# Hybrid convolution, attention and expert kernel on one core: experts of a half in one run, GpSimd weightings and dummy matmuls, another order of scan stage and batch norm

## What is computed

```python
# layer 0: convolution and two Mamba scans, one in each direction over the 256 tokens of an image
o = silu(depthwise_conv3x3(lin1(x)) + dw_b)
s = tokens(o) @ fc_in_w
o = (mamba(s, 0) + flip(mamba(flip(s), 1))) @ fc_out_w
o = (o - mu) * rsqrt(var + 1e-5) * bn_g + bn_b         # batch norm over images and pixels
x1 = sigmoid(conv1x1(o, conv4_w) + conv4_b) * x + x
# layer 1: causal attention on 256 tokens of 32 channels, one head
t = t + attention(layernorm(t))
# layer 2: mixture of 8 experts, the best two for each token
h = layernorm(t)
p = softmax(h @ router_w + router_b); top_p, top_i = top_k(p, 2); top_p /= sum(top_p)
t = t + sum_k top_p[k] * (h @ expert_w[top_i[k]] + expert_b[top_i[k]])
```

## Time and profile before

| | us |
|---|---|
| median of three runs | 103.01 |
| the three runs | 103.29, 98.75, 103.01 |
| profiled execution | 99.49 |
| its span, first to last instruction | 97.7 |
| PE busy | 87.1 |
| weight loads (PEld) busy | 54.5 |
| DVE busy | 47.3 |
| ACT busy | 34.8 |
| GpSimd busy | 16.6 |

### The profile page before, as it was taken

The page is one execution under the profiler, slowest core; times in us unless marked ns, Lnnn a source line. Parts: engine busy times, 40 slices in busy tenths (PEclk is TensorE's granted clock), DMA queues, the critical chain, the costliest instruction groups (busy, mean ns, idle before and its releaser), DMA issues.

```text
span 97.7 us, 1958 instructions
## 1 busy us (share of the span) xinstructions
PE 87.1 (89%) x793; PEld 54.5 (56%) x793; DVE 47.3 (48%) x116; ACT 34.8 (36%) x76; POOL 16.6 (17%) x31
## 2 busy tenths in 40 slices
PE   5999999999969979766988978999979999998990
PEld 1424465544456645533637654665546676995980
DVE  1420041956679578335334830641157999991000
ACT  5001282962280145453697214347424010001011
POOL 5000990007429500000000000000000009000000
PEclk9999999999999999998599999999999655555589
DMA  2699600000000000000000000000000000000000
GB/s 53 216 277 345 247 7 0 0 0 0 0 7 0 7 0 0 0 0 7 3 3 0 0 0 0 7 0 0 0 0 0 0 7 0 0 27 27 0 27 27
DMA packets 1620, 3.16 MB, mean 32 GB/s; under 512 B 198, under 2 KB 838, under 8 KB 1612
## 3 DMA queue, kind: packets, MB, share of 16 engines
q1 hardware_dynamic: 1612, 3.04, 9.8%
HBM read 2.78 MB, written 0.26 MB: 31 GB/s over the span
## 4 chain that ended last, share of the span: by engine, by line
PE 79%; ACT 11%; DVE 3%; DMA 2%; issue 2%; DVEq 0%
PE banks L560 8%; PE banks L883 8%; PE banks L912 8%; PE banks L530 5%; PE banks L597 4%; PE banks L902 3%; PE banks L679 3%; PE banks L615 2%; DMA pw<-in_pw 2%; PE banks L652 2%; PE banks L901 2%; PE banks L522 2%; PE banks L515 2%; PE banks L746 2%; PE banks L666 2%
## 5 line engine op out<-in xcount | busy, mean ns | idle before, releaser
L1000 DVE TENSOR_TENSOR_SCAN lmat<-banks,data 128x512 f32<-128x512 f32 x8 | 9.7, 1217 | 4.5 <-PE banks L597 4.4
L324 POOL TENSOR_TENSOR lmat<-lmat 128x512 f32<-128x512 f32 x2 | 2.5, 1290 | 47.6 <-DVE lmat L1209 47.6
L912 PE MATMUL banks<-pb,lmat 128*128 128x128 f32 x40 | 8.3, 386 | 0.0
L560 PE MATMUL banks<-o,fold_w 32*32 32x512 f32 x128 | 8.2, 596 | 0.0
L912 PEld LDWEIGHTS banks<-pb,lmat 128*128 128x128 f32 x40 | 8.1, 302 | 0.0
L883 PE MATMUL banks<-pd,h 32*128 32x256 f32 x32 | 7.8, 563 | 0.1
L515 PE MATMUL banks<-warm 128*128 128x512 bf16 x15 | 5.9, 524 | 1.2 <-DVE warm L960 1.2
L883 PEld LDWEIGHTS banks<-pd,h 32*128 32x128 f32 x32 | 5.5, 268 | 1.1 <-issue 0.7
L1006 DVE TENSOR_TENSOR mmat<-banks,lmat 128x512 f32<-128x512 f32 x8 | 5.0, 682 | 1.3 <-PE banks L615 1.3
L482 ACT ACTIVATE fin<-banks 128x128 f32<-128x128 f32 x4 | 1.1, 277 | 12.2 <-PE banks L912 12.2
L1209 DVE TENSOR_TENSOR lmat<-banks,wtok 128x256 f32<-128x256 f32 (+1 forms) x12 | 5.4, 504 | 0.1
(11 more groups left out here) (185 smaller groups left out, 165.8 us busy)
## 6 DMA issues: line engine op xcount, KB each, us to landing
im<-in_im SPq DMA_DIRECT2D x2, 445.5 KB
pc<-in_pc SPq DMA_DIRECT2D x1, 577.5 KB, 7.7
pb<-in_pb SPq DMA_DIRECT2D x1, 405.0 KB, 6.8
pd<-in_pd SPq DMA_DIRECT2D x1, 336.0 KB, 8.1
x<-in_x SPq DMA_DIRECT2D x1, 256.0 KB, 7.8
out<-fin SPq DMA_DIRECT2D x4, 64.0 KB, 1.6
pw<-in_pw SPq DMA_DIRECT2D x1, 100.2 KB, 2.2
pf<-in_pf SPq DMA_DIRECT2D x1, 80.0 KB, 6.3
```

What stands on the lines that cost most here:

```text
L560: mm = pe.matmul(proj_bank[2 * d + g][to:to + C, :], fold_w[r, 2 * d + g, k, :], o4[r, :, at:at + L], start=(k == 0), stop=(k == TAPS1 - 1))
L912: mm = pe.matmul(o, mix[:, k, e, :, :], packs["ident"], start=False, stop=(e == terms - 1))
L1000: dve.tensor_tensor_scan(lmat[:, i, :], dab_bank[i % 2][:, :], data1[:, d, :], 0.0, ALU.mult, ALU.add).then_inc(S["scanned"], 1)
```

## The change

**Scan stage.** PE issues the prefix rows and both turns of the first group behind the last projection instead of between projections; ACT does all four silu before the two copies. `products(1)` stands ahead of the second output, `states(1)` behind it. The fourth output's square moves from ACT to DVE, and `mean_squares(3)` and `gated(3)` stand earlier. The folds of the output weights stand behind the products for dt.

**Batch norm.** DVE subtracts the mean while it reads PSUM (`centred_o`), in place of ACT's copies. The weights are multiplied by `bn_g` early, on GpSimd; the shift's product with `bn_b` stands ahead of the statistics. Dummies: six ahead of the average, six behind it, five behind the gate matmuls (before: one, one, five, three).

**Experts' stage.** The bias is written into the four banks by four matmuls of one row, and the eight matmuls of a half follow in one run, block by block over four images. ACT copies half 0's four banks to `eout` in SBUF; half 1 waits for the copies. DVE weights images 0 and 1 of half 0 from `eout`, GpSimd images 2 and 3 by four products of 128x256; GpSimd's additions go, and half 0's blocks have eight products each. The bias by turned weights goes. Ties among experts are found by a running count (a scan of 128x64 with a reset) and one instruction, in place of a product, a maximum and a comparison. 18 dummies stand between these matmuls. One input pack is 64 columns wider.

Core of the diff:

```diff
-            for k in range(NC):
-                pool.wait_ge(S["mix_ready"], BQ)
-                pool.tensor_tensor(mix[:, k, 0:E // 2, :, :], mix[:, k, 0:E // 2, :, :], mix[:, k, E // 2:E, :, :], ALU.add)\
-                    .then_inc(S["summed"], 1)
+            w4 = wtok[:, 0, :, :].rearrange("p (k q) e -> p k q e", q=BQ)
+            for q in POOL_MIX:
+                pool.wait_ge(S["e_copied"], q + 1)
+                pool.wait_ge(S["w_ready"], 1)
+                for k in range(NC):
+                    m = pool.tensor_tensor(mix[:, k, :, q, :], eout[:, q, k, :, :],
+                                           w4[:, k, q, :].rearrange("p (e o) -> p e o", o=1).to_broadcast([P, E, C]), ALU.mult)
+                m.then_inc(S["pool_mixed"], 1)
...
             silu(0)
             silu(2)
+            silu(1)
+            silu(3)
             turned_copy(0)
             turned_copy(1)
-            silu(1)
-            silu(3)
...
-            square(3)
             rms(3)
-            for bh in range(BH):
-                act.wait_ge(S["bn_stats_done"], bh + 1)
-                act.activation(osb[:, bh, :], o_bank[bh][:, 0:L], ACT.Copy).then_inc(S["o_copied"], 1)
...
+            def expert_copy(q):
+                act.wait_ge(S["e_done"], 1)
+                act.activation(eout[:, q, :, :, :].rearrange("p k e c -> p (k e c)"), e_bank[q][:, :], ACT.Copy)\
+                   .then_inc(S["e_copied"], 1)
...
             inverse_sums(1)
+            expert_copy(0)
             ln2_square(1)
+            expert_copy(1)
             ln2_root(1)
             second_exp(0)
-            w_copy(0)
+            expert_copy(2)
+            expert_copy(3)
             second_exp(1)
             store_copy(0)
             store_copy(1)
-            w_copy(1)
...
-            prefix_rows(0)
             project(1, 0)
-            transposed(0)
             decays(3)
             project(1, 1)
-            transposed(1)
             decays(4)
             project(1, 2)
             decays(5)
             project(1, 3)
+            transposed(0)
             decays(6)
+            transposed(1)
+            prefix_rows(0)
             products(0)
             decays(7)
             states(0)
             skipped(0)
             outputs(0)
             prefix_rows(1)
+            products(1)
             skipped(1)
             outputs(1)
-            products(1)
...
+            mean_squares(3)
             mixer_out(0, 0)
             mixer_out(0, 1)
-            mean_squares(3)
             mixer_out(1, 0)
-            keep_warm(1, 0)
             mixer_out(1, 1)
-            keep_warm(1, 0)
+            pe.matmul(bank[7][:, 4:5], packs["conv4"], packs["bn_b"], start=True, stop=True)
+            keep_warm(6, 0)
             pe.wait_ge(S["bn_step"], 2)
             pe.matmul(bank[7][:, 0:2], packs["bn_avg"], bn_mv[:, :], start=True, stop=True).then_inc(S["bn_avg_done"], 1)
-            keep_warm(5, 6)
-            pe.wait_ge(S["bn_shift_ready"], 1)
-            pe.matmul(bank[7][:, 2:3], packs["conv4"], bn_v[:, 4:5], start=True, stop=True).then_inc(S["shift_done"], 1)
+            keep_warm(6, 0)
             pe.wait_ge(S["conv4_w_ready"], 1)
             pe.wait_ge(S["m_ready"], 8)
             for bh in range(BH):
-                pe.wait_ge(S["o_copied"], bh + 1)
+                pe.wait_ge(S["o_centred"], bh + 1)
                 pe.matmul(bank[2 + bh][:, 0:L], conv4_w[:, :], osb[:, bh, :], start=True, stop=True)\
                   .then_inc(S["conv4_done"], 1)
-            keep_warm(3, 6)
+            keep_warm(5, 0)
...
-            def experts(j):
-                q, bh = j % BQ, j // BQ
-                r = slice(C * q, C * q + C)
+            def expert_bias(bh):
+                if bh == 0:
+                    pe.wait_ge(S["prob_ready"], 4)
+                else:
+                    pe.wait_ge(S["e_copied"], BQ)
+                for q in range(BQ):
+                    r = slice(C * q, C * q + 1)
+                    pe.matmul(e_bank[q][:, :], ones[r, :],
+                              packs["experts_b"][r, :].rearrange("p (o n) -> p o n", o=1).to_broadcast([1, NC, E * C]),
+                              start=True, stop=False)
+            def experts(bh):
                 pe.wait_ge(S["h2_ready"], bh + 1)
-                if j == 0:
-                    pe.wait_ge(S["prob_ready"], 4)
-                if j >= 4:
-                    pe.wait_ge(S["mix_ready"], j - 3)
-                for i in range(2):
-                    mm = pe.matmul(e_bank[q][:, 256 * i:256 * i + 256], h2[r, bh, Q * i:Q * i + Q],
-                                   packs["experts"][r, :], start=True, stop=True)
+                for c in range(NC):
+                    for q in range(BQ):
+                        r = slice(C * q, C * q + C)
+                        mm = pe.matmul(e_bank[q][:, 256 * c:256 * c + 256], h2[r, bh, Q * c:Q * c + Q],
+                                       packs["experts"][r, :], start=False, stop=(c == NC - 1))
...
+            def opened(k):
+                bh, c = k // NC, k % NC
                 pe.wait_ge(S["t2_ready"], bh + 1)
                 pe.wait_ge(S["rest_ready"], bh + 1)
-                r = slice(32 * (k % NC), 32 * (k % NC) + 32)
-                pe.matmul(o, packs["experts_b"][r, :], wtt[r, bh, :], start=True, stop=False)
-                pe.matmul(o, packs["ident"], t2[:, bh, Q * (k % NC):Q * (k % NC) + Q], start=False, stop=False)
-                terms = E // 2
-                if bh == 0:
-                    pe.wait_ge(S["summed"], k + 1)
+                pe.matmul(mixed_bank[k][:, 0:Q], packs["ident"], t2[:, bh, Q * c:Q * c + Q], start=True, stop=False)
...
+            def mixed(k):
+                terms = E
+                if k < NC:
+                    pe.wait_ge(S["mix_ready"], len(DVE_MIX))
+                    pe.wait_ge(S["pool_mixed"], len(POOL_MIX))
                 elif k == NBLK - 1:
                     pe.wait_ge(S["last_summed"], 1)
+                    terms = E // 2
                 else:
-                    pe.wait_ge(S["mix_ready"], 2 * BQ)
-                    terms = E
+                    pe.wait_ge(S["mix_ready"], len(DVE_MIX) + BQ)
                 for e in range(terms):
-                    mm = pe.matmul(o, mix[:, k, e, :, :], packs["ident"], start=False, stop=(e == terms - 1))
+                    mm = pe.matmul(mixed_bank[k][:, 0:Q], mix[:, k, e, :, :], packs["ident"], start=False,
+                                   stop=(e == terms - 1))
...
+            expert_bias(0)
+            experts(0)
+            pe.wait_ge(S["l2_ready"], 1)
+            keep_warm(1, 7)
             centre2(1)
+            keep_warm(3, 7)
             variance2(1)
-            experts(0)
+            keep_warm(5, 7)
+            route_bias(1)
+            route(1)
+            keep_warm(3, 7)
+            expert_bias(1)
             experts(1)
-            route_bias(1)
-            experts(2)
-            route(1)
-            experts(3)
-            weights_turned(0)
-            experts(4)
-            experts(5)
-            experts(6)
-            experts(7)
+            keep_warm(6, 7)
+            opened(0)
+            opened(1)
             mixed(0)
             mixed(1)
-            weights_turned(1)
+            opened(2)
+            opened(3)
...
+            gated(3)
+            dve.wait_ge(S["yg_ready"], 4)
+            dve.tensor_tensor(ysq[:, 1, 1, :], yg[:, 1, 1, :], yg[:, 1, 1, :], ALU.mult).then_inc(S["ysq3_ready"], 1)
             normed(1)
-            gated(3)
...
+            def centred_o(bh):
+                dve.tensor_scalar(osb[:, bh, :], o_bank[bh][:, 0:L], bn_m[:, 0:1], None, ALU.subtract)\
+                   .then_inc(S["o_centred"], 1)
+            centred_o(0)
+            dve.wait_ge(S["halved"], 1)
+            dve.scalar_tensor_tensor(bn_v[:, 5:6], bank[7][:, 4:5], 0.5, b_half[:, :], ALU.mult, ALU.add)\
+               .then_inc(S["bias_ready"], 1)
+            dve.wait_ge(S["conv4_g_ready"], 1)
             dve.wait_ge(S["bn_rs"], 1)
-            dve.tensor_tensor(bn_v[:, 3:4], packs["bn_g"], bn_v[:, 2:3], ALU.mult).then_inc(S["bn_scale_ready"], 1)
-            dve.wait_ge(S["bn_scale_ready"], 1)
-            dve.scalar_tensor_tensor(bn_v[:, 4:5], bn_m[:, 0:1], bn_v[:, 3:4], packs["bn_b"], ALU.mult, ALU.subtract)\
-               .then_inc(S["bn_shift_ready"], 1)
-            dve.tensor_scalar(conv4_w[:, :], packs["conv4"], bn_v[:, 3:4], None, ALU.mult).then_inc(S["conv4_w_ready"], 1)
-            dve.wait_ge(S["shift_done"], 1)
-            dve.wait_ge(S["halved"], 1)
-            dve.scalar_tensor_tensor(bn_v[:, 5:6], bank[7][:, 2:3], -0.5, b_half[:, :], ALU.mult, ALU.add)\
-               .then_inc(S["bias_ready"], 1)
+            dve.tensor_scalar(conv4_w[:, :], conv4_g[:, :], bn_v[:, 2:3], None, ALU.mult).then_inc(S["conv4_w_ready"], 1)
+            centred_o(1)
...
```

(11 more changed lines are left out.)

120 lines of the change are left out of this document (49 added, 71 removed), and 3 rows, old and new, of the table names.

## The result

The changed kernel takes 96.11 us (four runs, 95.85 to 96.42); the kernel before, on the same chip, 98.75 to 103.29 us (four runs, median 101.25). The ratio is 0.970, interval 0.962 to 0.978: faster by 3%. The kernel before has executions near 99 and executions near 103; every ratio in this document is taken over the shorter of the executions of either kernel, and the four runs here, as will turn out, are all of the changed kernel's longer kind. The profiled execution took 96.21 us, its span is 94.4.

What follows compares the result with a forecast made beforehand. PE, with 79% of the chain, bounds the kernel, and its half clock sets 17 us. Span 97.7 - 1.1 - 5.1 = 91.5, time 93.3, plus 1.0 for a short half-clock stretch: 94.3 us, range 91.3 to 98.7.

Steps and rivals of the forecast that it cites:

- the starting point of the sum: Whole kernel: the old profiled execution's span, 97.7 us, from which the gains were subtracted; 1.79 us lie around it.
- Rival 4: Whole kernel: executions of the kind of 103 us dominate, giving 97 to 98 us; chance 0.08.
- Scan stage: Scan stage: moved turns cost 0.8 us, the square on DVE saves 1.25; -0.2 to -0.5, counted as zero.
- The wait of 0.9 us ahead of the second transposition: Scan stage: PE waits there for the first turned copy; its absence would show the forecast wrong.
- Batch norm: Batch norm: earlier shift matmul and DVE centring bring the layer norm's first square from 51.09 to 50.0; -1.1 us.
- Experts' stage: Experts' stage to the last mixing product: ends at 90.3 instead of 95.43, -5.1 us, at full clock.
- weights to mixing: Experts' stage: from half 0's weights at 78.5 to the mixing's start at 83.5.
- The alternation: Weighting: DVE and GpSimd take turns reading SBUF operands; of GpSimd's 2.5 us, 2.0 are lost to DVE.
- rival 2: Experts' stage: clock falls at 76.3 as before, returns early in the mixing; 97.1 us, chance 0.17.
- The added 1.0 us for one short stretch at half clock: Whole kernel: allowance for one half-clock stretch as short as the batch norm's 3.5 us, raising 93.3 to 94.3.
- Rival 1: Weighting: no loss between DVE and GpSimd, mixing starts at 81.8, 1.7 earlier; 91.6 us, chance 0.07.
- Rival 3: Experts' stage to the end: the clock falls and stays low, slower, ending at about 102 us; chance 0.10.

Runs made afterwards that it cites:

- before_dense: Kernel before with only four full-row dummies added directly behind the convolution; median 100.07 us, ratio 1.012.
- before_dense_warm: Kernel before with four dummies behind the convolution and 15 in the experts' stage; median 94.36 us, ratio 0.954.
- dve_all: Changed kernel with DVE weighting all four images of half 0 and GpSimd none; 92.53 to 96.67 us, median 95.12.
- dense_no_dummies: Changed kernel with folds ahead of the dt products and four dummies behind the convolution, without the experts' stage's 18 dummies; median 94.65 us, ratio 0.960.
- before_warm: Kernel before with 15 dummies between its expert matmuls, nothing else changed; 100.46, 96.94, 92.74 and 94.61 us.
- no_dummies: Changed kernel without the 18 dummies of the experts' stage; median 94.61 us, ratio 0.965.
- scan_before: Changed kernel with the scan stage's order of before, the last quarter's square still on DVE; 93.09 to 96.56 us, ratio 0.951.

## Why the prediction was right or wrong

**The step that failed is the starting point of the sum.** I took 97.7 us and subtracted; that counts everything ahead of the scan stage as unchanged, and the half clock at the start as lasting equally long. In the changed kernel's profiled execution the first decays came 3.69 us later for it, and all four executions of the result lie at the longer kind. Behind this stands a misread row: I took the clock as full but for two stretches, since PEclk prints 1.00 from the start. The pace shown above says otherwise, as 48 passes of 256 columns in the convolution take 5.28 us and 48 of 512 columns in the projections 2.74, so in the trace of before, too, the clock rose only between the two. The terms themselves gave 97.7 - 1.1 - 5.1 = 91.5 of span and 93.3 of time; the one execution of the changed kernel with the time of an early rise and a mean clock of 1.00 takes 92.53, so the other terms were 0.8 too small together. Rival 4, longer executions at some 4 us over 93.3, is the one that the result shows: right in kind (97 to 98 us, where 96.11 was measured because the other terms gave more), with a chance of 0.08 where it needed several times that. The times shown spoke for it: the median of the kernel before was 103.01 while its profile was of the 99 kind. Why the rise comes late in some executions stays open. That the executions of the kernel before near 103 are those with a late rise is likely, since none of the twelve with the four dummies has it, but none of them was traced.

**Scan stage**, -0.2 to -0.5, counted as zero: measured -0.29, made of +0.74 and some -1.0, where I had +0.8 and -1.25. The wait of 0.9 us ahead of the second transposition was named as a mark; it is there, with 0.98. That the dummies of the batch norm would swallow the gain was true of half of it (next point).

**Batch norm**, -1.1: measured -0.72, and for another reason than the reordering. In before_dense the clock did not fall there, and the old order is faster than the new one:

```profile
43.71 0.43 DVE yn L1028
...
46.39 0.17 DVE bn_m L1063
...
51.04 0.39 ACT c1sq L430
```

```profile
46.15 0.44 DVE yn L1037
...
48.98 0.17 DVE bn_m L1074
...
53.77 0.39 ACT c1sq L430
```

The first is 7.33 us, the second (changed) 7.62: 0.15 is lost at the average, where PE has six dummies queued ahead of it, and 0.14 between the average and the first square. So the term priced the clock, as the prediction half said ("most of this is the clock"), and by itself the new order, with its added dummies, costs 0.3 us. before_dense_warm shows the clock's price from the other side: there it fell from 46.65 to 50.06, and the old order took 8.32 us, like the 8.34 of before. The table load, which I had as the bound, was not what came last ahead of the gate: it ended at 51.26, the scaled matmuls at 51.5.

**Experts' stage**, -5.1 to the last product: measured -5.93 from the first square on. The parts: the run of the eight matmuls 0.87 (0.86 predicted); 28 products 6.5 us (6.4); weights to mixing 4.0 us where I had 5.0 (78.5 to 83.5). That term was mis-sized: DVE's own part is 2.7 (dve_all's 3.95 less two products of 0.62) where I had 3.0, and DVE lost 1.26 where I had 2.0. The alternation itself is in the trace. `pick` ends at 82.05, just behind GpSimd's first product (81.97), `is` at 84.24, just behind the fourth (84.16); the first weighting, issued at 81.97, ends 0.55 behind the second product (82.54), and the third product, beside that weighting, takes 1.06 where the others take 0.62 or 0.63. But only these three DVE instructions, each with two SBUF operands, were issued while a product ran; `rest` and the maximum read at most one operand from SBUF and take their 0.21 and 0.22, and `diff`, issued as the third product ended, takes its 0.17. I had charged the alternation to most of GpSimd's time. For the Trainium skill's page SBUF — State Buffer, section Who interferes with whom, this means: a DVE instruction with two SBUF inputs contends with GpSimd's reads, as it says, and these three agree; how many of them meet a product has to be counted one by one. (The 1.29 us that I read from the earlier trace rows is the mean of the two products there; the first took 1.26.)

**The cause of the gain** was put right: the clock. But I split it wrongly: the sum took the regrouping's gain to need a clock that its dummies hold, and rival 2 took most of it as lost if the clock falls. dense_no_dummies is as near to rival 2 as these runs come (without the dummies that stood in rival 2's sum): the clock fell at 78 and came back early in the mixing, and that cost 1.4 us of the stage, not the 3.8 that rival 2 had over 93.3. The added 1.0 us for one short stretch at half clock was right in size: the executions of the changed kernel with a mean clock of 0.98 lie 1.1 to 1.8 us above the one without. Rival 1, no loss between the engines, falls as stated, since 1.26 us were lost; but its 3.3 us from weights to mixing lie nearer to the measured 4.0 than my 5.0. Rival 3, half clock to the end, is in no execution of the changed kernel, as far as its times and mean clocks tell.

## What to carry to other kernels

Where a profile shows stretches at half clock, by its granted clock or by the pace of equal instructions, cost the change once with the clock held and once without, and test the clock by itself with dummies in the old kernel: here 15 idle matmuls gave the old kernel 5.3 of the 6.0 us that regrouping and dummies give together. Where the runs shown fall into two kinds, find out first which kind the profile is of, and give each kind its own sum. Work moved from DVE to GpSimd beside a busy DVE has to be priced with DVE's stretched instructions, and can come to nothing, as it did here.

## What the runs showed of the hardware that was not expected

The clock's first rise came at 9.6 to 12.5 us in some traces; in three others (the changed kernel twice, and dve_all) the pace of the projections puts it at 18.2 to 19.0, and in before_warm it came at 21.1. One and the same program shows both by its times, some 3.5 us of the whole. With the taps fold between the convolution's halves it came at 22.75 in the execution traced and the times of all twelve fit that; with four 128-row matmuls directly behind the convolution it came early in 28 of 28 executions by their times. What in the early work decides it (rows, gaps or the moment at which it starts) was not separated and stays open. So does what makes the clock fall for a short stretch in some executions and not in others: at 13 and 14 us in no_dummies and scan_before, whose first work is that of the changed kernel, and at 46 us in the kernel before and in before_dense_warm but not in before_dense, where PE's work in that stage is the same.
